# Paired transposes and a third half for the scores, a router in two groups, expert 0's weights ahead of routing, and head 0's queries copied on chip

## What is computed

```python
x = x + attention(norm(x), ctx, ctx)            # 16 heads of 32, causal, 2 x 1024 keys
x = x + moe(norm(x), gate_w, w1, w2, w3)        # 8 experts, top 2: silu(x w1) * (x w3), times w2
x = x + quant_attention(norm(x), ctx, Wq, Wkv, Wp)   # q, k, v and the softmax weights rounded to 8 bits
x = x + bitlinear_ffn(norm(x), w_gate, w_up, w_down) # rows to 8 bits, weights to -1, 0, 1
```

## Time and profile before

| what | us |
|---|---|
| median of three runs | 1657.66 |
| the profiled execution's own time | 1657.65 |
| its span, first to last instruction | 1655.9 |
| PE busy | 1417.4 |
| DVE busy | 1020.5 |
| ACT busy | 757.4 |
| POOL busy | 437.0 |

### The profile page before, as it was taken

The page is one execution under the profiler, slowest core; times in us unless marked ns, Lnnn a source line. Parts: engine busy times, 40 slices in busy tenths (PEclk is TensorE's granted clock), DMA queues, the critical chain, the costliest instruction groups (busy, mean ns, idle before and its releaser), DMA issues.

```text
span 1655.9 us, 23143 instructions
## 1 busy us (share of the span) xinstructions
PE 1417.4 (86%) x7965; PEld 683.2 (41%) x8012; DVE 1020.5 (62%) x1717; ACT 757.4 (46%) x1090; POOL 437.0 (26%) x324
## 2 busy tenths in 40 slices
PE   7993888888856999999999999667888888869778
PEld 3441555555544444444444444322323333324334
DVE  5998999999854011101111101677989999964995
ACT  4774888888810111111111111215777777762553
POOL 1114100000004768999910000311111111100341
PEclk9996999999958899999999999885555555559989
DMA  7997555564209999999987889369999999992001
GB/s 246 290 275 166 106 126 126 116 132 98 54 1 365 375 349 380 380 394 405 396 327 296 294 310 305 114 132 196 206 209 217 218 214 215 213 199 76 1 1 51
DMA packets 506455, 354.91 MB, mean 214 GB/s; under 512 B 419736, under 2 KB 421784, under 8 KB 505760
## 3 DMA queue, kind: packets, MB, share of 16 engines
q1 hardware_dynamic: 491744, 304.94, 68.4%
q0 software_dynamic: 10816, 40.90, 7.5%
q10 hardware_dynamic: 3840, 8.39, 1.3%
HBM read 206.06 MB, written 38.01 MB: 147 GB/s over the span
## 4 chain that ended last, share of the span: by engine, by line
PE 46%; DVE 23%; issue 13%; DMA 11%; ACT 4%; POOL 2%; DVEq 1%; POOLq 0%; ACTq 0%; SPq 0%
PE scores L974 17%; PE bank L992 9%; DVE arena L1757 8%; DMA arena<-arena 7%; PE bank L880 4%; PE bank L864 2%; DVE arena L1543 2%; DVE arena L1529 2%; PE bank L863 2%; ACT arena L1261 2%; PE bank L1166 1%; PE bank L984 1%; POOL xs_d L689 1%; POOL arena L750 1%; DMA qst_d<-arena 1%
## 5 line engine op out<-in xcount | busy, mean ns | idle before, releaser
L1757 DVE TENSOR_SCALAR_CACHE_REDUCE arena<-scores,arena 128x1024 f32<-128x1024 f32 x256 | 318.3, 1281 | 30.3 <-PE scores L1040 25.7
L974 PE MATMUL scores<-arena 128*128 128x512 f32 x736 | 321.4, 595 | 4.3 <-DMA arena<-in_L_ffn_w 4.3
L1332 ACT ACTIVATE arena<-arena 128x2048 int16<-128x2048 f32 x128 | 256.2, 2002 | 130.8 <-POOL arena L765 93.1
L1689 DVE TENSOR_TENSOR arena<-scores,arena 128x512 f32<-128x512 f32 x46 | 31.8, 692 | 449.7 <-PE scores L974 449.7
L1040 PE MATMUL scores<-arena 96*128 96x512 bf16 x512 | 261.0, 620 | 54.4 <-DVE arena L1757 30.4
L974 PEld LDWEIGHTS scores<-arena 128*128 128x128 f32 x736 | 140.4, 191 | 181.1 <-issue 181.1
L992 PE MATMUL bank<-arena 128*128 128x512 f32 x368 | 165.0, 601 | 3.4 <-issue 3.3
L1529 DVE TENSOR_REDUCE arena<-scores 128x1 f32<-128x640 f32 (+3 forms) x128 | 127.7, 1018 | 8.1 <-PE scores L841 7.7
L1261 ACT ACTIVATE arena<-bank 128x512 f32<-128x512 f32 (+3 forms) x256 | 116.8, 507 | 25.8 <-PE bank L864 25.8
L1543 DVE TENSOR_TENSOR arena<-arena 128x1024 f16<-128x1024 f32 (+2 forms) x128 | 126.2, 1026 | 3.5 <-issue 1.8
L1289 ACT ACTIVATE arena<-scores 128x512 f32<-128x512 f32 x46 | 27.5, 597 | 215.7 <-PE scores L974 215.7
(11 more groups left out here) (268 smaller groups left out, 2061.1 us busy)
## 6 DMA issues: line engine op xcount, KB each, us to landing
arena<-in_L_ffn_w SPq DMA_DIRECT2D x69, 2048.0 KB, 12.5
arena<-arena SPq DMA_DIRECT2D x32, 256.0 KB, 3.0
kst_d<-arena POOLq DMA_DIRECT2D x16, 384.0 KB, 6.5
tern_d<-arena POOLq DMA_DIRECT2D x12, 512.0 KB, 7.0
arena<-kst_d SPq DMA_DIRECT2D x16, 384.0 KB, 4.2
xs_d<-arena SPq DMA_DIRECT2D x23, 256.0 KB, 3.5
arena<-xs_d SPq DMA_DIRECT2D x22, 256.0 KB, 12.9
ys_d<-arena ACTq DMA_DIRECT2D x22, 256.0 KB, 7.0
```

Of the source, the lines that this page charges most:

```text
L974: ins = pe.matmul(scores[:, m * 1024 + half * 512:m * 1024 + half * 512 + 512], xsT[a][:, c], wa[:, m, c, half * 512:half * 512 + 512], st ...
L1332: act.activation(p16[t % PBUF], ssb[i], ACT.Exp, bias=ebias[i], scale=-1.0, accum_out=rsum[a][:, t:t + 1]).then_inc(p_ready, 1)
L1757: dve.tensor_scalar(ssb[i][:, s:s + 1024], scores[:, s:s + 1024], nsq[:, bass.ds(h, 1), t], None, ALU.mult, ALU.min, accum_out=nmx[i][:, h ...
```

## The change

- **Router in two groups.** The adds, the statistics and the norm are done for tiles 0 to 3, then for tiles 4 to 7 (`norm_group`). PE turns four tiles, makes their logits with the roles of the operands exchanged (4 float32 matmuls of 512 columns, result 8 x 512), then the other four. ACT copies the 8 x 512 result to `lgT` and PE turns it back in 8 small transposes. One step of the routing chain is gone (`R_SLOTS` 29 to 28).
- **Expert 0 first.** Expert 0 always has slot 0, so its 6 MB are loaded when DVE has made its first add of the attention's result. After routing, SP begins with slot 1's weights.
- **Ternary transposes earlier.** The two 2 MB transposes are issued ahead of the loads for slots 20 and 21.
- **Queries.** Four buffers of `q3row` and `qTbuf` in place of two. SP stores the tiles to `qst_d` itself, and copies head 0's part (96 x 128) from `qTbuf` straight to `qhead`; PE waits for it tile by tile.
- **Scores in three halves**, six PSUM banks; `ssb` has three buffers in place of four.
- **Pairs.** One transposing DMA of 1 MB moves two tiles. There are three pairs of `p16` and two pairs of `pT`. PE does the value matmuls of two tiles together, behind the scores of tile n = 2j + 7 for pair j. The loops over heads are written out.

```diff
-PBUF = 4
-LAG = 3
+PAIRS_P, PAIRS_T = 3, 2
 SCALE = float(HD) ** -0.5
 LN_EPS, RMS_EPS = 1e-5, 1e-6
-SBUFS = 4
+SBUFS = 3
...
-        scores = stack.enter_context(nc.psum_tensor("scores", [P, 4 * 512], F32))
-        bank4 = stack.enter_context(nc.psum_tensor("bank4", [P, 512], F32))
-        bank5 = stack.enter_context(nc.psum_tensor("bank5", [P, 512], F32))
+        scores = stack.enter_context(nc.psum_tensor("scores", [P, 6 * 512], F32))
+        bank4, bank5 = scores[:, 2048:2560], scores[:, 2560:3072]
...
-        p16 = [r.take(I16, B * SK) for r in (rq, rq, over_xn3, over_xn3)]
-        pT = [r.take(F16, NC, P) for r in (rq, rq, over_xn3, over_xn3)]
+        p16_at = rq.at
+        p16 = [r.take(I16, 2, B * SK) for r in (rq, over_xn3, over_xn3)]
+        pT = [rq.take(F16, 2, NC, P)]
...
+        ssb.append(over_q3.take(F32, B * SK))
+        pT.append(Region(early.start).take(F16, 2, NC, P))
+        over_p16, over_pT = Region(p16_at, p16_at + 8 * 1024), Region(p16_at + 8 * 1024, p16_at + 16 * 1024)
+        q3row += [over_p16.take(BF16, H, 3, HD) for _ in range(2)]
+        qTbuf += [over_pT.take(BF16, 3 * HD * H // P, P) for _ in range(2)]
...
+            sp.wait_ge(att_added, 1)
+            for m, w in enumerate((w1, w3)):
+                sp.dma_start(wbuf[0][0][:, m], w[0].rearrange("(k p) n -> p k n", p=P)).then_inc(w13_loaded[0], 16)
+            sp.dma_start(wbuf[0][1], w2[0].rearrange("(k p) n -> p k n", p=P)).then_inc(w2_loaded[0], 16)
             sp.wait_ge(r_step, R_SLOTS)
             with sp.register("expert") as expert:
                 def load_slot(u, a, k, first, last):
+                    if first:
+                        return
+                    if isinstance(u, int) and u in (SLOTS - 3, SLOTS - 2):
+                        w = u - (SLOTS - 3)
+                        for s in tern_stored:
+                            sp.wait_ge(s, 16 * 6)
+                        sp.dma_start_transpose(wT[w].rearrange("p o c n -> p (o c) n"), tern_d[w]).then_inc(wT_in, 16)
...
-                sweep(sp, SLOTS, load_slot)
-            for a in range(2):
-                sp.wait_ge(tern_stored[a], 16 * 6)
+                sweep(sp, SLOTS, load_slot, 3)
             sp.dma_start(wq_sb, Wq.rearrange("(k p) n -> p k n", p=P)).then_inc(wq_loaded, 16)
             sp.dma_start(bq_row, bq.partition_broadcast(P)).then_inc(wq_loaded, 16)
-            for w in range(2):
-                sp.dma_start_transpose(wT[w].rearrange("p o c n -> p (o c) n"), tern_d[w]).then_inc(wT_in, 16)
...
+            q_rows = qst_d.rearrange("h r n -> (h r) n").rearrange("(m p) n -> p m n", p=P)
+            def stage_q(u):
+                sp.wait_ge(kT_in[u % 2], 16 * (NC // 2 + u // 2 + 1))
+                if u >= 2:
+                    sp.wait_ge(q0_in[u % 2], 16 * (u // 2))
+                    sp.wait_ge(qst_stored[u % 2], 16 * (u // 2))
+                sp.dma_start(qhead[0][0:K3, u * P:(u + 1) * P], qTbuf[u % 4][0:K3, 0]).then_inc(q0_in[u % 2], 16)
+                sp.dma_start(q_rows[:, :, u * P:(u + 1) * P], qTbuf[u % 4]).then_inc(qst_stored[u % 2], 16)
             for u in range(NT):
                 sp.wait_ge(q3_ready, u + 1)
-                if u >= 2:
-                    sp.wait_ge(qst_stored[u % 2], 16 * (u // 2))
-                sp.dma_start_transpose(qTbuf[u % 2], q3row[u % 2].rearrange("p h c d -> p (h c d)")).then_inc(kT_in[u % 2], 16)
+                if u >= 4:
+                    sp.wait_ge(qst_stored[u % 2], 16 * (u // 2 - 1))
+                    sp.wait_ge(q0_in[u % 2], 16 * (u // 2 - 1))
+                sp.dma_start_transpose(qTbuf[u % 4], q3row[u % 4].rearrange("p h c d -> p (h c d)")).then_inc(kT_in[u % 2], 16)
+                if u:
+                    stage_q(u - 1)
+            stage_q(NT - 1)
             for a in range(2):
                 sp.wait_ge(qst_stored[a], 16 * (NT // 2))
-            load_queries(0)
...
-            for n in range(H * NT):
-                i = n % PBUF
-                if n >= PBUF:
-                    sp.wait_ge(av_done, n - PBUF + 1)
-                sp.wait_ge(p_ready, n + 1)
-                sp.dma_start_transpose(pT[i], p16[i].bitcast(F16)).then_inc(pT_in[i], 16)
-                h, t = divmod(n, NT)
-                if t == NT - 1 and h + 2 < H:
+            for j in range(H * NT // 2):
+                i = j % PAIRS_T
+                if j >= PAIRS_T:
+                    sp.wait_ge(av_done, 2 * (j - PAIRS_T + 1))
+                sp.wait_ge(p_ready, 2 * j + 2)
+                sp.dma_start_transpose(pT[i].rearrange("p o c n -> p (o c) n"),
+                                       p16[j % PAIRS_P].rearrange("p o n -> p (o n)").bitcast(F16)).then_inc(pT_in[i], 16)
+                h, pair = divmod(j, NT // 2)
+                if pair == NT // 2 - 1 and h + 2 < H:
...
-            q_rows = qst_d.rearrange("h r n -> (h r) n").rearrange("(m p) n -> p m n", p=P)
-            for u in range(NT):
-                pool.wait_ge(kT_in[u % 2], 16 * (NC // 2 + u // 2 + 1))
-                pool.dma_start(q_rows[:, :, u * P:(u + 1) * P], qTbuf[u % 2]).then_inc(qst_stored[u % 2], 16)
...
-            turn_rows(pe, xn, ln_step, LN_STEPS * 2 - NT, xn_turned, xT_ready, (bank4, bank5), idf)
-            pe.wait_ge(att_added, NT + 1)
-            pe.wait_ge(xT_ready, NT)
-            for t in range(NT):
+            pe.wait_ge(xT_ready, 1)
+            def turn_xn(t):
+                pe.wait_ge(ln_step, LN_APPLIED[t // GT] + t + 1)
+                if t >= 2:
+                    pe.wait_ge(xT_ready, t if t <= GT + 1 else t + 1)
+                bank = (bank4, bank5)[t % 2]
                 for c in range(KC):
-                    ins = pe.matmul(bank7[:, t * E:(t + 1) * E], XT[:, c, t * P:(t + 1) * P], gwT[:, c], start=c == 0, stop=c == KC - 1)
-            ins.then_inc(logits_done, 1)
+                    ins = pe.transpose(bank[:, c * P:(c + 1) * P], xn[:, t, c * P:(c + 1) * P], idf)
+                ins.then_inc(xn_turned, 1)
+            def group_logits(g):
+                pe.wait_ge(xT_ready, GT + 1 if g == 0 else NT + 2)
+                for c in range(KC):
+                    ins = pe.matmul(scores[0:E, g * 512:(g + 1) * 512], gwT[:, c], XT[:, c, g * 512:(g + 1) * 512], start=c == 0, stop=c == KC - 1)
+                ins.then_inc(logits_done, 1)
+            def turn_logits(g):
+                pe.wait_ge(xT_ready, GT + 2 if g == 0 else NT + 3)
+                for t in range(g * GT, (g + 1) * GT):
+                    ins = pe.transpose(bank7[:, t * E:(t + 1) * E], lgT[0:E, t * P:(t + 1) * P], idf[0:E, 0:E])
+                ins.then_inc(logits_done, 1)
+            for t in range(GT):
+                turn_xn(t)
+            group_logits(0)
+            for t in range(GT, NT):
+                turn_xn(t)
+            turn_logits(0)
+            group_logits(1)
+            turn_logits(1)
...
-            def a1_scores(h, a, t, first):
-                for half in range(2):
-                    if not first:
-                        pe.wait_ge(s_read, 2 * (8 * h + t) + half - 1)
+            def a1_scores(n):
+                h, t = divmod(n, NT)
+                if t == 0:
+                    pe.wait_ge(k_loaded[h % 2], 32 * (h // 2 + 1) - 16 * (1 - h % 2))
+                if h == 0:
+                    pe.wait_ge(q0_in[t % 2], 16 * (t // 2 + 1))
+                for m in (2 * n, 2 * n + 1):
+                    if m >= 3:
+                        pe.wait_ge(s_read, m - 2)
                     for j in range(2):
-                        s = half * 1024 + j * 512
-                        ins = pe.matmul(scores[:, s:s + 512], qhead[a][0:K3, t * P:(t + 1) * P], khead[a][0:K3, s:s + 512], start=True, stop=True)
+                        s, k = (m % 3) * 1024 + j * 512, (m % 2) * 1024 + j * 512
+                        ins = pe.matmul(scores[:, s:s + 512], qhead[h % 2][0:K3, t * P:(t + 1) * P], khead[h % 2][0:K3, k:k + 512], start=True, stop=True)
...
+            def a1_pv(n):
+                h, t = divmod(n, NT)
+                j = n // 2
+                bank = (bank6, bank7)[h % 2]
+                if t % 2 == 0:
+                    pe.wait_ge(pT_in[j % PAIRS_T], 16 * (j // PAIRS_T + 1))
...
+            for n in range(H * NT):
+                a1_scores(n)
+                if n % 2 and n >= 7:
+                    a1_pv(n - 7)
+                    a1_pv(n - 6)
+            for n in range(H * NT - 6, H * NT):
+                a1_pv(n)
...
+            def exp_tile(n):
+                h, t = divmod(n, NT)
+                j = n // 2
+                if n % 2 == 0 and j >= PAIRS_P:
+                    act.wait_ge(pT_in[(j - PAIRS_P) % PAIRS_T], 16 * ((j - PAIRS_P) // PAIRS_T + 1))
+                if t == 0 and h >= 2:
                     act.wait_ge(a_post, 3 * (h - 1))
                 act.wait_ge(bias_ready, n + 1)
-                act.activation(p16[t % PBUF], ssb[i], ACT.Exp, bias=ebias[i], scale=-1.0, accum_out=rsum[a][:, t:t + 1]).then_inc(p_ready, 1)
```

(33 more changed lines are left out.)

170 lines of the change are left out of this document (70 added, 100 removed).

## The result

The changed kernel took 1630.62 us (median of four runs, 1629.12 to 1632.69); the kernel before, beside it, 1657.72. The ratio is 0.984, with a 95% interval of 0.9825 to 0.9854: 1.6% faster. The forecast was 1611 and the range 1593 to 1632, so the time lies at the range's slow end, and 9 us beyond rival B (1622).

A forecast was written before the change was run, and what follows sets the result against it. It took PE to bound expert slots and DVE, PE and DMA to be near full in attention, with DMA pacing the changed loop. 1657.65 - 17.5 (router) - 3.5 (store) - 25.5 (queries and loop) = 1611 us; range 1593 to 1632.

The forecast's parts named there:

- rival B: Attention loop keeps 22.1 us a head, transfers already at their limit or DVE waiting for `p_ready`; 1622 us, chance 0.18.
- Router and slots 0 and 1: Shorter logits and early expert 0 weights let slot 1's first matmul start 17.5 us sooner (15.7 to 18.4).
- Slot 21's store: At the experts' end, earlier ternary transposes cut store-to-gather from 6.58 to about 3 us: -3.5 (0 to -4.5).
- Queries: Before the attention loop, DVE's first score read comes up to 17.5 us sooner; transposed data flow from about 1124.8.
- The loop, 21.4 a head: DMA paces attention at 21.4 us a head, where it was 22.1; queries and loop together give -25.5 us.
- the mishaps: Slot 20 or 21 waits 8 us or more, or slot 1's rows stay late, atop B: 1625 to 1650, chance 0.07.
- Rival A: DVE paces the attention loop because the DMA queues can carry more than 213 GB/s; 1597 us, chance 0.20.
- Rival C: In the attention loop, pair transposes serialize with two `pT` buffers, losing the saving; 1658 us and up, chance 0.03.

The follow-up runs named there:

- a_tern_late: The changed kernel with the two 2 MB ternary transposes issued behind the last expert's weights, as before the change: 1633.34 us.
- a_half_bytes: The changed kernel with each pair's DMA transposing only its first tile (512 KB instead of 1 MB), used for both tiles' values: 1587.61 us.
- a_no_loads: The changed kernel without the loads of keys and queries for heads 2 to 15, which use stale ones: 1598.66 us.
- d_old4: The changed kernel with the old attention loop's buffers, places, two halves, order and one DMA a tile, but heads still written out: 1636.12 us.
- singles: The changed kernel with each pair moved by two DMAs of 512 KB, the first issued once the pair's first tile is ready: 1640.08 us.

## Why the prediction came out as it did

- **Router and slots 0 and 1, -17.5.** Measured -20.6 by span and -21.1 from the first add. The parts: logits 7.5 for the 5.2 taken, since the second group ran at 0.45 us a record (3.60 over 8), the lower of the two prices; slot 0's start 8.8 sooner for 6.7. From PE's wait to slot 1's matmul 8.76 us, taken as 8.7, and the rows were in time. The mechanism was right; the size is 2 us beyond the fast bound. One reading was off: in the earlier trace rows 1.08 us is two of ACT's copies together, and what slot 0 now waits for last is DVE's copy (L1735), behind a reciprocal of 3.35 us.
- **Slot 21's store, -3.5.** Measured -3.7 (6.58 to 2.86). Right; the trace of a_tern_late agrees (7.19), and shows that the slots hide the transposes. Its time, 2.7 slower, is not clear of the noise.
- **Queries, -17.5.** First read 41.2 earlier, of which 24.3 were there at the first gather: 16.9. Right. The first pair landed at 1105.4, which in before's time (24.3 later) is 1129.7; data flowing from 1124.8 and 4.8 us for a pair give the same.
- **The loop, 21.4 a head.** This step failed, and the miss is here: the stage's end came at 1465.06 + 24.3 = 1489.4 in before's time, not at 1465.0, and the 3 us that the router gave beyond the forecast hide a little of that. A head took 22.9, outside the 20.9 to 21.9 that the prediction had set itself. That DMA paces the loop was right (a_half_bytes, a_no_loads); what it can carry was not. I had taken 213 GB/s for the transposes alone and then let keys and queries pass at 307, 1.7 to 1.9 us a head. But 213 is the mean over both the earlier trace rows: 4.78 MB at it are 22.4 us. The runs give the same from the parts: eight undisturbed transposes at 2.51 are 20.1, and a_no_loads has 2.3 for the loads, or a little more, since it reached DVE's floor. The text itself had the sentence ("DMA can't go faster than the loop went") and the sum passed over it. That is 0.7 us of the 1.5 a head if held against the 22.1 of before, 1.0 by 22.4: 11 to 16 us in all. The rest is the fall from 213 to 209 GB/s, which no step of the prediction had: it looked at what the edits do to waits, not that the loops of PE, ACT and DVE were written out, and that this is the cause is argued only. The last 2 us are DVE's final wait, 12.59 for 10.65.
- **That the time fell within the range is luck.** The range reached 1632 for the mild end of the mishaps, a late weight or row on top of B (1625 to 1650). No such mishap came, and no case of the prediction had queues that carry less than before.
- **What paced the kernel before** is less clear than the sum took it. A tile costs DVE 1.35 + 1.20 us and finishing a head about 1.3, so 21.7 of the 22.1 a head are DVE's with two halves, and from 1230 to 1430 us PE waited only 6.1 us for transposes (19.8 in d_old4, 48.1 in the changed kernel). So DVE's limit lay within half a us of the head's time too. What a third half gives to a register loop no run shows.
- **Rival A** (DVE paces, 1597) would have needed queues with room. a_half_bytes shows it would have come true with less to move. By the rule of the Trainium skill that a transposing DMA is as fast as another (Advanced Engine Details and Errata, X-Bar Transpose (TRN2)) there was such room. No loop here carried more than 217 GB/s over 40 us, so for this kernel the rule does not hold.
- **Rival B** (22.1 kept, 1622) came nearer, by the first of its two reasons: transfers at their limit already. It is the forecast with its arithmetic put right, and 0.18 was too little for it; even so the loop is 0.8 us a head slower than B.
- **Rival C** (pairs serialize) did not come: pairs issue in 5.20 us (median) and are 9.5 us better than singles. (Its "saved 42 us" should be the 38.5 that it divides.)

## What to carry to other kernels

When the share of the DMA engines is above 1 and the rate doesn't change from slice to slice, divide the bytes of a period by that rate before believing any gain on an engine; a mean over mixed traffic may not be split and one part of it made faster. Then ask of a change to the loop how many bytes it takes away: buffers, halves and order took away none. Where transfers pace a loop, look at the queues of kind "instruction" in both kernels, since the written-out loops here had 17 to 19 such packets in 200 us where the register loop had 2, and the diff doesn't show them. And before asking what one resource would give, ask how near the next one is: here DMA and DVE were almost level.

## What the runs showed that was not expected

- With a packet of kind "instruction" (8 or 16 KB) on the way a transpose lands 1.3 us later (3.81 for 2.52 in d_old4), of which the next landing gives about half back, though such packets are half a per cent of the bytes (0.32 of 58.4 MB from 1150 to 1430 us in the changed kernel).
- One transposing DMA of 1 MB for two tiles was better than two of 512 KB by 9.5 us over the 64 pairs of the loop.
- The granted clock of PE in the loop (1150 to 1430 us) rose with three halves: its mean was 0.69 in the changed kernel and 0.68 in a_half_bytes, but 0.51 with two halves (PE busy 194, 212 and 230 of 280 us) and 0.50, the lower level of 1.2 GHz, before. Score matmuls took 544 ns on average in the changed kernel, 620 before. It gave nothing here, as PE was not the bound.
- Distance between scores and values on PE: three tiles in place of five cost 34 us.
